# Task places shifted engine by engine, and the value products of two quads issued back to back

## The chip, the cores and the metric

The kernel runs on one core of one Trainium2 chip. The metric is the device time of one execution in microseconds (us). A core has TensorE (PE, matrix products into PSUM banks), VectorE (DVE), ScalarE (ACT), GpSimd (POOL) and SyncE (SP, which here only issues DMAs). The engines run side by side and meet through semaphores.

## The reference, cut to what matters

Two transformer layers over 8 sequences of 512 tokens, width 256, 16 heads of 16.

```python
# layer 1
q, k, v = split(x @ Wqkv);  q, k = rope(q), rope(k);  q, k = q / norm(q), k / norm(k)
x = layernorm(x + softmax(q @ k.T / 4) @ v @ Wo + bo)
# layer 2
h = layernorm(x) * ln1_w + ln1_b
x2 = x + softmax(q2 @ k2.T / 4) @ v2 @ w_proj        # q2, k2, v2 = split(h @ w_qkv)
e = argmax((layernorm(x2) * ln2_w + ln2_b) @ gate_w + gate_b)
x2 = x2 + gelu(h2 @ w1[e]) @ w2[e]                   # one expert of 8 for each token
out = layernorm(x + x2)
```

In layer 1 q and k have norm 1, so the exponentials need no maximum taken off. In layer 2 each row's largest score is found first and taken off inside the score product.

## The kernel before, in words

A sequence and a layer make a batch: batches 0 to 7 are layer 1, 8 to 15 layer 2. The program runs in 18 stages. In stage n, batch n is projected, batch n-1 attended, batch n-2 finished (output projection, norms, gate). After that a tail of 39 tiles runs the experts.

A stage has 16 quads of 4 steps; a step is written quad.step, as 5.3. In each step PE issues one score product of 128 keys by 512 queries (`score`, L417) into one of four PSUM banks (three in layer 2), and ACT takes its exponential (`exp`, L632) into `probs`. PE may issue score c only when the exponential four (in layer 2, three) steps back is done. In step 1 of every quad PE issues the value product of the quad two places earlier (`pv`, L434): four products that each use 32 columns of the array, fp32, so that the trace shows eight records for a set. All sixteen quads of a batch go to one bank, which ACT empties once in four quads (L641).

For layer 2 a maximum tile stands behind each score from quad 10 of the batch's own stage on, six quads ahead of its use: PE issues `max_score` (L449) into one of two banks and DVE reduces it (`max_tile`, L835). Every 16 tiles DVE splits the maxima into three bf16 parts (`neg_split`, L850 to L857), PE transposes them (task `NG`, L507), ACT copies them (L694), and SP sends them by DMA into the score operand (L1297). The scores of the next four quads wait for that DMA.

All else is tasks, placed by hand. The tables `PROJECTED`, `ATTENDED` and `FINISHED` give each task's (quad, step), apart for layer 1 and layer 2. At each step every engine runs its part of the tasks that stand there, behind its score, exponential or maximum; ACT runs its part one step later. The tasks that matter here:

- `T0`, `T1`: x is transposed for the projections. `qA`, `qB`, `kA`, `kB`: halves of q and k (PE L478, one PSUM bank for all projection tasks, so each waits until the one before is read out). In layer 2 ACT copies the bank to bf16 (L655) and DVE subtracts that copy from the bank (L967), which frees it.
- `sq`, `nq`, `sk`, `nk`: layer 1 only. ACT squares q or k (L664), PE sums over each head (L485), ACT takes the logarithm and the exponential of it (L671, L674).
- `mq`, `mk` (layer 2): the middle bf16 part on ACT (L680), the low part on POOL (L1182), and then 12 DMAs each on SP (L1283) that lay q and k out for the scores.
- `V0`, `V1` the values, `TO`, `TP`, `WO` the attention output, `R` the reciprocal deviations on ACT, `N1`, `N2` the norms, `HT`, `GT`, `RT` gate and routing.

Of the kernel before, what the change touches and what calls it, by code (L numbers as in the profile page):

```python
# [15 lines left out]
BATCH, T, D, H = 8, 512, 256, 16  # L16
# [38 lines left out]

PROJECTED = (
    dict(T0=(0, 0), T1=(0, 2), qA=(1, 3), qB=(2, 2), kA=(3, 3), kB=(4, 2), sq=(4, 3), nq=(5, 3),
         sk=(6, 1), uq=(6, 2), hq=(6, 3), nk=(7, 0), lq=(7, 1), uk=(8, 1), hk=(8, 2), lk=(9, 0),
         V0=(12, 0), V1=(14, 0)),
    dict(T0=(0, 0), T1=(0, 2), qA=(1, 2), qB=(2, 1), kA=(3, 0), mq=(3, 0), kB=(3, 3), mk=(4, 2),  # L60
# [5 lines left out]
    dict(TO3=(2, 3), TP0=(4, 0), TP1=(6, 3), WO0=(9, 3), WO1=(10, 2), R1=(11, 2), N10=(12, 0),  # L66
         N11=(12, 2), R2=(13, 2), N20=(14, 0), N21=(14, 2)),
    dict(TO3=(2, 3), TP0=(4, 0), TP1=(4, 3), WO0=(5, 3), WO1=(7, 0), R2=(8, 0), N20=(8, 2),
         N21=(9, 0), HT0=(10, 3), GT0=(11, 1), HT1=(12, 1), GT1=(12, 3), RT=(14, 0)))
PROJ_BANK = ("T0", "T1", "qA", "qB", "kA", "kB", "nq", "nk", "V0", "V1")  # L70
# [4 lines left out]
def second(b):  # L75
    return b >= BATCH
# [8 lines left out]
def tasks(n, q, j):  # L85

    projected, attended, finished = batches(n)
    found = []
    for b, places in ((finished, FINISHED), (attended, ATTENDED), (projected, PROJECTED)):
        if b is not None:  # L90
            found += [(name, b) for name, at in places[second(b)].items() if at == (q, j)]
    return found
# [41 lines left out]
def program(nc, x, w_qkv1, w_o1, b_o, ln1_w, ln1_b, w_qkv2, w_o2, ln2_w, ln2_b, gate_w, gate_b,  # L134
# [5 lines left out]
    with ctx:  # L140
# [193 lines left out]
        for n in range(STAGES):  # L334
            for q in range(QUADS):
                for j in range(HEADS_AT_ONCE):
                    for name, b in tasks(n, q, j):
# [48 lines left out]
        def pv_quad(n, q):  # L386

            projected, attended, finished = batches(n)
            if q < 2:
                return [] if finished is None else [(finished, QUADS - 2 + q)]  # L390
            return [] if attended is None else [(attended, q - 2)]
# [9 lines left out]
        def _(pe):  # L401
# [21 lines left out]
            def pv(b, q):  # L423

                if q == 0:
                    pe.wait_ge(*p_ring.empty(b, "V0"))
                    pe.wait_ge(*p_ring.empty(b, "V1"))
                g, kt = q // TT, q % TT
                pe.wait_ge(exps, CHUNKS * b + HEADS_AT_ONCE * (q + 1))
                if kt == 0:  # L430
                    wait(pe, oT_ready, GROUPS * b + g)
                for j in range(HEADS_AT_ONCE):
                    at = (kt * H + HEADS_AT_ONCE * g + j) * VS
# [934 lines left out]
```

## Time and profile before

| | us |
|---|---|
| median of 3 runs | 1537.66 (1533.43 to 1538.38) |
| the profiled execution, its own time | 1548.81 |
| its span, first to last instruction | 1546.8 |
| stages 2 to 7 (six, layer 1 only), each | 54.5 to 56.5 |
| stages 9 to 15 (seven, maxima in every quad), each | 78.3 to 93.1 |
| stage 16 | 67.7 |
| from the last score to the end (experts) | 371.7 |

How to read it: the stages are cut at the first score of each. A busy PE in a row counts a product from its issue to its modelled end, so the starts of two rows tell more than their lengths. "[2.12 <-DVE negm L835]" behind a row is the engine's idle time just before it and what ended it.

### The profile page before, as it was taken

What the parts mean: (1) busy time and instruction counts of PE and PEld (TensorE: products, weight loads), DVE (VectorE), ACT (ScalarE), POOL (GpSimd) and SP (SyncE); (2) the same over time, 40 slices, a digit from 0 to 9 for tenths busy, and PEclk for the clock granted to TensorE, in tenths of its full rate; (3) what the DMA queues carried; (4) which work ended last, traced back from release to release, by engine and by line L of the source; (5) the groups of instructions that cost most, each with busy time, mean ns of one, the idle gap of its engine ahead of it and who ended that gap; (6) DMA issues with size and microseconds to landing.
All of it is one profiled execution on the core that took longest, in us unless ns stands there. A gap on an engine that the chain in (4) does not pass through costs nothing. (4 is left out here: it accounts for less than half of the span.)

```text
span 1546.8 us, 20966 instructions
## 1 busy us (share of the span) xinstructions
PE 1330.6 (86%) x7238; PEld 694.1 (45%) x7238; DVE 794.6 (51%) x1815; ACT 921.1 (60%) x1617; POOL 311.7 (20%) x247
## 2 busy tenths in 40 slices
PE   3499999999998887888989899898985399999994
PEld 1223433443343323333434333333332399999993
DVE  3333553554452656566767575767761333433431
ACT  0277777787776554546556565556653167777773
POOL 4122222323321111111212121212111211111110
PEclk9699999999999998899999999999998599999997
DMA  6221431331332121112222121212236511111113
GB/s 179 81 77 47 137 94 54 127 118 59 97 123 96 42 96 42 53 45 69 69 56 83 56 83 42 96 43 83 69 111 224 170 42 53 52 52 56 52 52 129
DMA packets 103495, 127.87 MB, mean 83 GB/s; under 512 B 7168, under 2 KB 91008, under 8 KB 103264
## 3 DMA queue, kind: packets, MB, share of 16 engines
q1 hardware_dynamic: 71568, 79.45, 16.3%
q10 hardware_dynamic: 27392, 33.56, 7.3%
q0 software_dynamic: 4432, 13.52, 2.5%
q8 instruction: 60, 0.98, 0.3%
q14 instruction: 43, 0.35, 0.1%
HBM read 51.51 MB, written 28.46 MB: 52 GB/s over the span
## 5 line engine op out<-in xcount | busy, mean ns | idle before, releaser
L632 ACT ACTIVATE w_space<-bank 128x512 f32<-128x512 f32 x1024 | 565.3, 598 | 423.1 <-PE bank L417 420.1
L417 PE MATMUL bank<-w_space 96*128 96x512 bf16 (+1 forms) x1024 | 358.3, 388 | 36.3 <-DMA w_space<-neg_T 18.7
L835 DVE TENSOR_REDUCE negm<-bank 128x1 f32<-128x512 f32 x512 | 326.9, 682 | 95.6 <-PE bank L449 93.8
L434 PE MATMUL bank<-w_space 128*32 128x512 f32 x2048 | 281.4, 623 | 3.3 <-ACT w_space L641 3.3
L449 PE MATMUL bank<-w_space 96*128 96x512 bf16 x512 | 200.9, 392 | 47.0 <-DVE negm L835 40.2
L417 PEld LDWEIGHTS bank<-w_space 96*128 96x128 bf16 (+1 forms) x1024 | 94.4, 100 | 295.1 <-ACT w_space L632 176.9
L605 PE MATMUL bank<-w_space,work_space 128*128 x624 | 141.7, 380 | 0.0
L478 PE MATMUL bank<-work_space,wqkv_sb 128*128 128x512 f32 x256 | 134.7, 652 | 7.2 <-DVE w_space L962 4.8
L1182 POOL TENSOR_TENSOR work_space<-w_space,work_space 128x1024 bf16<-128x1024 f32 x32 | 68.3, 2133 | 282.0 <-ACT work_space L680 191.5
L605 PEld LDWEIGHTS bank<-w_space,work_space 128*128 128x128 f32 x624 | 115.5, 190 | 14.4
L449 PEld LDWEIGHTS bank<-w_space 96*128 96x128 bf16 x512 | 50.4, 98 | 152.5 <-DVE negm L835 115.8
L1238 POOL DMA_INDIRECT out_rows<-rows_sb,work_space x39 | 37.5, 963 | 266.8 <-DVE rows_sb L1132 266.8
L434 PEld LDWEIGHTS bank<-w_space 128*32 128x32 f32 x2048 | 40.9, 109 | 101.4 <-issue 80.3
L1216 POOL TENSOR_TENSOR row_sb<-row_sb,rows_sb 128x512 f32<-128x512 f32 x32 | 37.9, 1184 | 228.7 <-DVE row_sb L943 228.7
L592 PEld LDWEIGHTS bank<-work_space 128*128 128x128 f32 x640 | 76.7, 197 | 1.9 <-DVE work_space L1105 0.9
L592 PE MATMUL bank<-work_space 128*128 128x128 f32 x640 | 77.0, 280 | 0.5 <-DVE work_space L1105 0.5
L478 PEld LDWEIGHTS bank<-work_space,wqkv_sb 128*128 128x128 f32 x256 | 50.7, 204 | 52.5 <-issue 35.1
L967 DVE TENSOR_TENSOR w_space<-bank,work_space 128x512 f32<-128x512 f32 x32 | 22.1, 691 | 99.7 <-ACT work_space L655 99.7
L592 PEld LDWEIGHTS bank<-work_space,wqkv_sb 128*128 128x128 f32 x608 | 70.8, 192 | 1.7 <-DVE work_space L1105 0.8
L592 PE MATMUL bank<-work_space,wqkv_sb 128*128 128x128 f32 x608 | 71.1, 275 | 0.5 <-DVE work_space L1105 0.5
L1118 DVE TENSOR_TENSOR wqkv_sb<-bank,work_space 128x256 f32<-128x256 f32 x39 | 16.6, 424 | 105.0 <-PE bank L605 104.9
L492 PE MATMUL bank<-wqkv_sb,work_space 128*128 128x256 f32 x256 | 63.3, 391 | 2.7 <-DVE w_space L975 1.9
(131 smaller groups left out, 1506.9 us busy)
## 6 DMA issues: line engine op xcount, KB each, us to landing
w_space<-work_space SPq DMA_DIRECT2D x384, 128.0 KB
w_space<-in_w_dram ACTq DMA_DIRECT2D x16, 1024.0 KB, 8.4
work_space<-rows_dram SPq DMA_DIRECT2D x39, 256.5 KB, 2.6
work_space<-in_x_dram ACTq DMA_DIRECT2D x16, 512.0 KB, 3.9
x_dram<-xo SPq DMA_DIRECT2D x16, 256.0 KB, 4.7
h_dram<-row_sb SPq DMA_DIRECT2D x16, 256.0 KB, 2.3
work_space<-h_dram ACTq DMA_DIRECT2D x8, 512.0 KB, 4.1
work_space<-x_dram ACTq DMA_DIRECT2D x8, 512.0 KB, 5.5
```

The source lines that it names most:

```text
L417: nc.tensor.matmul(bank[:, :], k_stack[0:rows, b % 2, HEADS_AT_ONCE * g + j, kt * P:(kt + 1) * P], q_stack[0:rows, b % 2, HEADS_AT_ONCE * ...
L434: last = nc.tensor.matmul(pv_bank[VW * j:VW * (j + 1), :], v_aug[:, b % 2, at:at + VW], probs[:, q % PROBS, j, :], start=(kt == 0), stop=( ...
L449: nc.tensor.matmul(mx_ring.bank(b, (g, c))[:, :], q_stack[0:STACK, b % 2, h, qt * P:(qt + 1) * P], k_stack[0:STACK, b % 2, h, :], start=Tr ...
L478: last = nc.tensor.matmul(bank[:, :], wqkv_sb[:, second(b), k, c * P:(c + 1) * P], xT[:, k, :], start=(k == 0), stop=(k == KD - 1))
L492: last = nc.tensor.matmul(bank[:, j * D:(j + 1) * D], xT[:, k, tt * P:(tt + 1) * P], wqkv_sb[:, second(b), k, 2 * D:3 * D], start=(k == 0) ...
L592: last = nc.tensor.matmul(psum[2 * (j % 2) + n][:, f * P:(f + 1) * P], w1_tile[j % 2][:, k, at:at + P], xsT[:, j % 2, k, :], start=(k == 0 ...
L605: last = nc.tensor.matmul(psum[5 + j % 2][:, 0:D], hidT[:, j % 2, k, :], w2_sb[:, bass.ds(e, 1), k, :].rearrange("p a d -> p (a d)"), star ...
L632: nc.scalar.activation(probs[:, q % PROBS, j, :], st_bank(b, c)[0][:, :], ACT.Exp, scale=SCALE).then_inc(exps, 1)
L835: ve.tensor_reduce(negm[:, c % TT, c // TT:c // TT + 1], mx_ring.bank(b, (g, c))[:, :], axis=AX.X, op=ALU.max, negate=True).then_inc(mx_ri ...
L1182: pool.tensor_tensor(parts[:, qk, 2, :, :], rest[:, qk, :, :], parts[:, qk, 1, :, :], ALU.subtract).then_inc(parts_ready, 1)
L1216: pool.tensor_tensor(both, both, rows_sb[:, r:r + 1, :].to_broadcast([P, 2, D]), ALU.mult).then_inc(hw_step, 1)
L1238: pool.indirect_dma_start(out_rows, bass.IndirectOffsetOnAxis(rows_in[:, j % ROWS_AHEAD, 2 * D:ROW].bitcast(U32), 0), o_sb[:, s, :], None) ...
```

## The change

Three things change.

First, `tasks` takes a table of lags for the engine that asks, and a task may be placed in the stage before or behind its own (the loops run from -1 to 18). ACT's lag of one step is now written as a table. In layer 2 DVE runs its part of `qA`, `qB`, `kA`, `kB` three steps behind the table's place, and SP its part of `mk` three steps behind.

Second, places move. Layer 1: `sq`, `sk`, `R1`, `R2` one step earlier. Layer 2: `T0`, `T1` into quads 14 and 15 of the stage before; `qA` 1.2 to 0.2, `qB` 2.1 to 1.3, `kA` 3.0 to 3.1, `kB` 3.3 to 4.3, `mk` 4.2 to 6.0.

Third, `pv` takes a pair of quads. It stands in quads 1, 3, 5, ... 15 and issues both sets without anything between them.

```diff
-    dict(T0=(0, 0), T1=(0, 2), qA=(1, 2), qB=(2, 1), kA=(3, 0), mq=(3, 0), kB=(3, 3), mk=(4, 2),
+    dict(T0=(-2, 2), T1=(-1, 2), qA=(0, 2), qB=(1, 3), kA=(3, 1), mq=(3, 0), kB=(4, 3), mk=(6, 0),
...
+ACT_LAG = (dict(other=1), dict(other=1))
+DVE_LAG = (dict(other=0), dict(qA=3, qB=3, kA=3, kB=3, other=0))
+SP_LAG = (dict(other=0), dict(mk=3, other=0))
...
-            if q < 2:
-                return [] if finished is None else [(finished, QUADS - 2 + q)]
-            return [] if attended is None else [(attended, q - 2)]
+            if q == 1:
+                return [] if finished is None else [(finished, QUADS // 2 - 1)]
+            return [] if attended is None or q % 2 == 0 else [(attended, (q - 3) // 2)]
...
-                g, kt = q // TT, q % TT
-                pe.wait_ge(exps, CHUNKS * b + HEADS_AT_ONCE * (q + 1))
+                for q in (2 * pair, 2 * pair + 1):
+                    g, kt = q // TT, q % TT
+                    pe.wait_ge(exps, CHUNKS * b + HEADS_AT_ONCE * (q + 1))
```

The line numbers of the changed kernel are higher by 8 to 12: scores are L427, value products L445, maxima L461 (PE) and L843 (DVE), the subtraction L975, the layout DMAs L1291, the DMAs of the maxima L1305.

PE, layer 1, quads 5 to 7, from one value product over `nq` (head_sum_sb), `TP1` (on) and `nk` to the next ones. Before:

```order
L434 MATMUL bank<-w_space 32x512 x4
L417 MATMUL bank<-w_space 128x512 x2
L485 MATMUL bank<-work_space,head_sum_sb 128x512 x2
L417 MATMUL bank<-w_space 128x512 x2
L434 MATMUL bank<-w_space 32x512 x4
L417 MATMUL bank<-w_space 128x512 x2
L515 MATMUL bank<-ident_sb,on 128x128 x4
L417 MATMUL bank<-w_space 128x512
L485 MATMUL bank<-work_space,head_sum_sb 128x512 x2
L417 MATMUL bank<-w_space 128x512
L434 MATMUL bank<-w_space 32x512 x4
```

Now:

```order
L445 MATMUL bank<-w_space 32x512 x8
L427 MATMUL bank<-w_space 128x512 x2
L497 MATMUL bank<-work_space,head_sum_sb 128x512 x2
L427 MATMUL bank<-w_space 128x512 x4
L527 MATMUL bank<-ident_sb,on 128x128 x4
L427 MATMUL bank<-w_space 128x512
L497 MATMUL bank<-work_space,head_sum_sb 128x512 x2
L427 MATMUL bank<-w_space 128x512
L445 MATMUL bank<-w_space 32x512 x8
```

The set of four value products that stood between `nq` and `nk` has gone behind `nk`.

DVE, layer 2, quads 0 to 3 of a stage, from the task of the attention output (recip, on) over the first two subtractions (w_space<-bank,work_space) and the split of the maxima. Before:

```order
L990 TENSOR_TENSOR on<-bank,recip 128x4x64
L835 TENSOR_REDUCE negm<-bank 128x1 x7
L967 TENSOR_TENSOR w_space<-bank,work_space 128x512
L835 TENSOR_REDUCE negm<-bank 128x1
L850 CAST neg_parts<-negm 128x4x4
L852 TENSOR_TENSOR neg_rest<-negm,neg_parts 128x16
L855 CAST neg_parts<-neg_rest 128x4x4
L857 TENSOR_TENSOR neg_parts<-neg_rest,neg_parts 128x4x4
L835 TENSOR_REDUCE negm<-bank 128x1 x2
L967 TENSOR_TENSOR w_space<-bank,work_space 128x512
```

Now:

```order
L998 TENSOR_TENSOR on<-bank,recip 128x4x64
L843 TENSOR_REDUCE negm<-bank 128x1 x6
L975 TENSOR_TENSOR w_space<-bank,work_space 128x512
L843 TENSOR_REDUCE negm<-bank 128x1 x2
L858 CAST neg_parts<-negm 128x4x4
L860 TENSOR_TENSOR neg_rest<-negm,neg_parts 128x16
L863 CAST neg_parts<-neg_rest 128x4x4
L865 TENSOR_TENSOR neg_parts<-neg_rest,neg_parts 128x4x4
L843 TENSOR_REDUCE negm<-bank 128x1 x3
L975 TENSOR_TENSOR w_space<-bank,work_space 128x512
```

On DVE the subtractions hardly move (1.2 to 1.1, 2.1 to 2.2). What has moved is the product that they read, three steps ahead of them on PE.

SP in a layer 2 stage, the layout DMAs (w_space<-work_space) and those of the maxima (w_space<-neg_T), over two stages. Before:

```order
L1297 DMA w_space<-neg_T 3x4x512 x2
L1283 DMA w_space<-work_space 8x16x512 x24
L1297 DMA w_space<-neg_T 3x4x512 x4
L1283 DMA w_space<-work_space 8x16x512 x24
L1297 DMA w_space<-neg_T 3x4x512 x4
```

Now:

```order
L1305 DMA w_space<-neg_T 3x4x512 x2
L1291 DMA w_space<-work_space 8x16x512 x12
L1305 DMA w_space<-neg_T 3x4x512
L1291 DMA w_space<-work_space 8x16x512 x12
L1305 DMA w_space<-neg_T 3x4x512 x3
L1291 DMA w_space<-work_space 8x16x512 x12
L1305 DMA w_space<-neg_T 3x4x512
```

The third DMA of the maxima (`NG2`) now stands between the 12 of `mq` and the 12 of `mk`.

## Rows read from the trace of the kernel before

**Rows 1.** Page, part 1: busy time, share of the span, instructions.
```profile
PE 1330.6 (86%) x7238; PEld 694.1 (45%) x7238; DVE 794.6 (51%) x1815; ACT 921.1 (60%) x1617; POOL 311.7 (20%) x247
```

**Rows 2.** Windows: stretch, length, busy time by engine, clock; stages 2-7, 13, 15, tail.
```profile
123.22:454.05 330.83, 318.14 (x1683) 130.65 (x1682) 165.77 (x396) 250.54 (x481) 96.31 (x65) 0.99 0.29 94
...
864.33:946.40 82.07, 74.20 (x383) 30.34 (x382) 55.42 (x125) 46.97 (x89) 15.84 (x14) 0.96 0.21 65
...
1029.11:1107.45 78.34, 70.77 (x381) 29.49 (x382) 54.75 (x124) 46.69 (x88) 15.58 (x14) 1.00 0.20 62
...
1175.15:1546.80 371.65, 305.36 (x2023) 280.63 (x2015) 132.80 (x327) 214.27 (x279) 50.35 (x53) 0.91 0.28 87
```

**Rows 3.** Timeline, stage 5: start, length, instruction, count, idle time before it.
```profile
309.30 1.07 PE L434 MATMUL bank<-w_space 128*32 128x512 f32 x8
...
310.30 0.60 PE L417 MATMUL bank<-w_space 96*128 96x512 bf16 x2
...
311.15 1.96 PE L485 MATMUL bank<-work_space,head_sum_sb 128*128 128x512 f32 x4 [0.24 <-ACT work_space L664]
...
316.06 1.06 ACT L664 ACTIVATE work_space<-w_space 128x1024 f32<-128x1024 f32 x1
...
317.26 1.10 PE L485 MATMUL bank<-work_space,head_sum_sb 128*128 128x512 f32 x2 [1.53 <-ACT work_space L664]
```

**Rows 4.** Timeline of PE, end of stage 16: one set of value products, then two sets.
```profile
1172.64 1.07 PE L434 MATMUL bank<-w_space 128*32 128x512 f32 x8
...
1174.61 1.92 PE L434 MATMUL bank<-w_space 128*32 128x512 f32 x16
```

**Rows 5.** Waits over the whole span: total, times, longest.
```profile
DVE w_space L967 <- ACT work_space L655: 99.7, 32, 7.5
...
PE bank L449 <- DVE negm L835: 40.2, 44, 2.1
...
PE bank L417 <- DMA w_space<-neg_T: 18.7, 11, 4.7
```

**Rows 6.** Timeline, stage 13, quads 1 and 2.
```profile
873.88 0.38 PE L417 MATMUL bank<-w_space 99*128 99x512 bf16 x1
...
874.39 0.60 ACT L655 ACTIVATE work_space<-bank 128x512 bf16<-128x512 f32 x1
...
875.03 0.69 DVE L967 TENSOR_TENSOR w_space<-bank,work_space 128x512 f32<-128x512 f32 x1 [2.85 <-ACT work_space L655]
...
876.37 0.61 PE L449 MATMUL bank<-w_space 96*128 96x512 bf16 x1 [2.12 <-DVE negm L835]
```

**Rows 7.** Timeline of PE, first score of stage 4.
```profile
234.21 0.52 PE L417 MATMUL bank<-w_space 96*128 96x512 bf16 x1 [1.87 <-issue]
```

**Rows 8.** Windows behind four waits of PE: length, busy times, clock third from the end.
```profile
234.30:237.70 3.40, 3.40 (x14) 1.17 (x13) 0.69 (x1) 1.19 (x2) 0.00 (x0) 0.50 0.50 175
317.20:320.60 3.40, 3.34 (x15) 1.05 (x16) 1.87 (x4) 2.51 (x5) 1.45 (x1) 1.00 0.00 0
568.80:575.60 6.80, 4.37 (x14) 1.05 (x15) 1.38 (x2) 1.24 (x3) 0.00 (x0) 0.50 0.13 47
...
876.10:882.80 6.70, 6.43 (x18) 2.16 (x19) 2.12 (x7) 0.00 (x0) 0.00 (x0) 0.50 0.01 2
```

**Rows 9.** Timeline, stage 13, quad 6.
```profile
902.60 1.06 PE L434 MATMUL bank<-w_space 128*32 128x512 f32 x8
...
903.51 0.40 DVE L850 CAST neg_parts<-negm 128x16 bf16<-128x16 f32 x1
...
904.68 0.38 PE L507 MATMUL bank<-ident_bf,neg_parts 128*12 128x128 bf16 x4 [1.02 <-DVE neg_parts L857]
```

**Rows 10.** Timeline, stage 13, SP's DMA issues (SPq) and the score of step 8.0.
```profile
892.76 16.39 SPq L1283 DMA_DIRECT2D w_space<-work_space  x24
909.20 0.76 SPq L1297 DMA_DIRECT2D w_space<-neg_T  x1
...
912.49 0.39 PE L417 MATMUL bank<-w_space 99*128 99x512 bf16 x1 [0.69 <-DMA w_space<-neg_T]
```

## What I predict, and why

> **What bounds the kernel now.** I read the totals first, then the windows by stage, then the timelines around PE's longest waits. PE is busy for 86% of the span [rows 1]. In the six stages 2 to 7 it is busy for 318.1 of 330.8 us, at clock 0.99 [rows 2], and ACT for 250.5: layer 1 is bound by PE, and what counts there is how long each set on PE takes. A stage of layer 2 takes 78.3 us (stage 15) to 82.1 (stage 13), with DVE at 55 us [rows 2]. It is bound by no one engine: PE stops for DVE and for a DMA. The waits name them, 40.2 us for a maximum tile and 18.7 us for the DMA of the maxima [rows 5]. The tail of 371.7 us [rows 2] is the experts. Nothing of it changes, and I leave it out.
>
> **Part 1, the subtraction behind its product (gain).** In stage 13 ACT copies `qA` at 874.39, and DVE, which stands at its subtraction, does it at 875.03 after 2.85 us idle, and only then the maximum behind it. PE sits from its score at 873.88 until 876.37, 2.12 us idle, since both banks of the maxima are full [rows 6]. Over the run DVE stands so for 99.7 us before its 32 subtractions [rows 5]. All seven stages 9 to 15 show this wait, with 2.11 or 2.12 us: 14.8 us. The three other subtractions have smaller ones; of the 40.2 us [rows 5] I give them 10. The product is now three or more steps ahead of its subtraction, with a pair of value products between, so the copy is ready. What is late next is DVE itself, at some 0.61 us a tile (2.47 us for four of them would be its pace), and I keep 3 us for it. Gain 22 us.
>
> **The clock behind that wait (gain).** Behind the wait of stage 13 the granted clock is 0.50 for 6.7 us [rows 8], so products run at 1.2 GHz and not at 2.4. Stage 15 has the same wait without the fall and is 82.1 - 78.3 = 3.7 us shorter [rows 2]. Stage 14 is as stage 13; stages 9, 10 and 12 have one fall of 3.4 us each, at half pace 1.7 us. Sum 3.4 + 3.4 + 5.1 = 12 us.
>
> **Part 2, the DMA of the maxima ahead of mk (gain).** SP issues the 24 layout DMAs in one run from 892.76 to 909.15, and only then the DMA of the third group (`NG2`); the score of step 8.0 waits for it until 912.49 [rows 10]. The waits at step 8.0 are 4.7, 2.5, 1.3, 0.6, 0.7, 1.2 and 0.7 us in stages 9 to 15, 11.8 us of the 18.7 [rows 5]. With `NG2` before the twelve of `mk` it is issued some 8 us earlier, so all of it goes: 11.5 us. Behind the two longest the clock is 0.50 for 6.8 us each [rows 8]; PE is partly idle there, so I take 5 us for both.
>
> What that costs: the twelve DMAs of `mk` leave later. They take half of 16.4 us, 8.2, and the last of them lands about 3.3 us after its issue if it does as that of the maxima (909.20 to 912.49) [rows 10]. Quad 10 needs them. Counted from `WO0` at 5.3, I put SP's start at 7.5 us (DVE's sum, POOL's sum and low part, then `NG2`), so 7.5 + 8.2 + 3.3 = 19.0, and PE's arrival at 10.0 at 21. It fits with 2 us to spare, at nothing. If PE came as early as its bare sets allow, at about 18.4, it would wait 0.6 us a stage.
>
> `T0` and `T1` go to quads 14 and 15. In quad 14 PE already waits for DVE, so `T0` (0.44 us) is free there; 3 us in all.
>
> **Part 3, the pairs.** A single set starts at 309.30 and the next score at 310.30 [rows 3]; the step into it costs another 0.09 over the normal 0.22. So it takes 1.09 us of PE. In stage 16 two sets happen to stand together: 1.92 us against 1.07, the second one costs 0.85 [rows 4]. A pair saves 0.24 us where PE is what bounds. The Trainium skill, "TensorEngine Tiling (Array Packing)", Key Properties, says that a change of tiling mode drains the array. The trace agrees with 1.00 against 0.85; taken alone, the rule would promise 128 x 0.24 = 31 us, and I take less, because of the following.
>
> The pair leaves every even quad without a value product, and in some of them the single one lay in a wait. Layer 1: between `nq` at 311.15 and `nk` at 317.26 PE waits 1.53 us for ACT's square [rows 3]. `nk` can't start before that square, which now comes one exponential (about 0.5 us) earlier: 5.6 us behind `nq` and not 6.1. The value set has left that stretch, so PE waits about 1.53 + 1.09 - 0.5 = 2.1 to 2.2 us, and pays 0.85 for it later. Net cost 0.4. In quads 7 to 9 there is too little else and ACT (0.49 us for one exponential of a run) binds: cost 0.5. The six other pairs gain 6 x 0.24 = 1.4, and the 0.24 us wait of `nq` goes [rows 3]. Net gain 0.9 us a stage, 7 us for eight.
>
> Layer 2: in quad 6 the split on DVE is started at 903.51 and `NG2` waits for it until 904.68, 1.02 us behind the value set [rows 9]. Without the set it still starts then, after 2.0 us of idle PE, and the set is paid again in quad 7: 0.85. Quads 10 and 14 have a split as well: 0.8 each. Five pairs gain 5 x 0.24 = 1.2. Net cost 1.3 us a stage, 11 us for eight and a half.
>
> **Part 4, the clock behind the new waits (cost).** No row shows the new waits; these are the nearest. The wait of 1.53 us in layer 1 keeps its clock at 1.00 [rows 8] in all of stages 2 to 7. The one of 1.87 us at the start of stage 4 [rows 7] is followed by 0.50 for 3.4 us [rows 8], and of 14 waits of 1.87 us or more before 1130 us, 11 are, for 3.4 or 6.8 us. The new waits of 2.1 and 2.0 us lie with these. Fifteen of them (seven in layer 1, eight in layer 2) at 11 in 14 are 12 falls of about 2.5 us; from that 29 us I take 20, since in quad 6 and 7 of layer 2 DVE holds PE back anyway. Bounds: 0 (no fall) and 15 x 3.4 = 51 us (each one long and PE bound throughout). The Trainium skill, "TensorE: Matmul & The Clock Gate", in the section on oscillation, tells of kernels in which short bursts between waits make the array start slow each time. The falls in these rows agree with it, and the sum does not need it.
>
> **Sum.** -22 - 12 - 11.5 - 5 - 3 + 11 - 7 = -49.5 without new falls, +20 with them: -29.5. From the profiled execution, 1548.8 - 29.5 = 1519.3. The median of the runs is 11.1 us lower than that execution: 1508 us.
>
> **Rivals.** (A) The new waits leave the clock alone, as the 2.12 us of stage 15 did, or turn out shorter: -49.5, so 1488 us. For it: three of 14 waits. Against: eleven. (B) Slower: the clock. Not one but several even quads of each stage (6, 10 and 14 in layer 2, 6 and 7 in layer 1) now hold a wait near 2 us, and a fall of 6.8 us costs 3.4. It decides from 49.5 / 3.4 = 15 long falls on; at 23 it stands at -49.5 + 78, so 1566 us. For it: 6.7 us at 0.50 in stages 13 and 14. Against: DVE's pace, which hides a slow product in layer 2, and the waits that go. (C) `mk` is late at 10.0 by 2 us in eight stages: 1508 + 16 = 1524 us. For it: the margin of 2 us; against: PE slows in the same quads. (D) DVE binds layer 2: with maxima, splits and sums DVE is at 55 of 78 us [rows 2], and in quads without value products PE can be no more than two tiles ahead of it. Then the waits only change places, and the time is that of before, 1538 us. (E) The pair doesn't save what the two sets of rows 4 show, because another quad's weights have to come: 100 pairs at 0.2 less: 1528 us.
>
> **How the numbers follow.** Forecast, with some falls (1495 to 1520): 0.38. A: 0.30. C: 0.07. E: 0.05. D: 0.06. B: 0.14. I predict 1508 us. The range goes from 10 us under A, 1478, to just over D, 1540; what it leaves out is most of B and a little below A. A measurement of this kernel can tell about 0.3% from no change. Faster by more than that: forecast, A, C and E, 0.80; within it: D, 0.06; slower: B, 0.14.
>
> **What would show it.** In the profile of the changed kernel: no wait for a maximum near 2 us in quad 2 and none for the DMA of the maxima at step 8.0; DVE's idle time before the subtraction down from 99.7 us to under 20; two sets of value products in 1.92 us; `nk` about 5.6 us behind `nq` with 2.1 us idle before it; `NG2` behind 2 us of idle; the clock at 0.50 for 3.4 us or more behind about twelve of these. Stages of layer 1 should take 53 to 55 us and stages 11 to 15 76 to 79. It is wrong if the clock falls in every stage (B), if quad 10 waits for `mk` (C), or if layer 2 stages stay at 80 with DVE waiting for nothing (D).

## The result, and the profile after

| | before | after |
|---|---|---|
| median of 5 runs each | 1535.2 (1528.19 to 1538.38) | 1545.88 (1544.61 to 1547.21) |
| ratio, 95% interval | 1 | 1.0075 [1.0047, 1.0104] |
| span of the profiled execution | 1546.8 | 1544.0 |
| stage 5 (layer 1) | 54.5 | 57.4 |
| stages 11 to 15 (layer 2), each | 78.3 to 82.7 | 78.9 to 80.6 |

The kernel became 0.75% slower, some 11 us, where I had predicted 1508 us and a range from 1478 to 1540. The profiled execution of before was 14 us above this median, so the two spans hide the loss; I go by stages and by medians. Page of after, part 1, then its windows (stages 2 to 7, 13, 15 and the tail; columns as in [rows 2]):

```profile
PE 1314.5 (85%) x7238; PEld 716.5 (46%) x7238; DVE 802.6 (52%) x1815; ACT 913.6 (59%) x1617; POOL 311.4 (20%) x247
```

```profile
125.28:467.87 342.59, 319.45 (x1690) 139.91 (x1688) 162.98 (x396) 250.15 (x483) 97.90 (x66) 0.98 0.28 92
866.23:945.45 79.22, 70.23 (x384) 31.29 (x382) 56.92 (x124) 46.05 (x89) 15.81 (x14) 0.98 0.23 68
1026.00:1104.87 78.87, 69.40 (x376) 30.63 (x373) 56.69 (x124) 45.66 (x88) 15.52 (x14) 0.98 0.21 60
1173.27:1544.00 370.73, 304.78 (x2029) 280.27 (x2027) 133.29 (x328) 215.36 (x281) 51.16 (x54) 0.91 0.28 88
```

The six stages of layer 1 grew from 330.8 to 342.6 us [rows 2]. Stage 1, also of layer 1, grew by 4.2. Stages 9 to 15, in which the sum had its gains, went from 582.6 to 564.0, 18.6 less, and stages 8 and 16 grew by 2 us each. The tail is as before. What was to leave did leave. Waits of after over the whole span (total, times, longest):

```profile
PE bank L519 <- DVE neg_parts L865: 33.0, 17, 3.8
PE bank L461 <- DVE negm L843: 31.4, 46, 1.7
...
PE bank L497 <- ACT work_space L676: 17.7, 8, 2.5
...
DVE w_space L975 <- ACT work_space L667: 16.5, 4, 5.2
...
PE bank L427 <- DMA w_space<-neg_T: 2.5, 3, 1.4
```

DVE's idle time before the subtractions is 16.5 us and not 99.7, the scores' wait for the DMA of the maxima 2.5 and not 18.7 [rows 5]. SP's issues in stage 13 show why: the DMA of the third group now goes out ahead of the twelve of `mk`.

```profile
884.20 7.99 SPq L1291 DMA_DIRECT2D w_space<-work_space  x12
902.85 0.76 SPq L1305 DMA_DIRECT2D w_space<-neg_T  x1
903.71 8.50 SPq L1291 DMA_DIRECT2D w_space<-work_space  x12
```

In their place stands 33.0 us for the split (L519 is the transpose of `NG`). Of it 22.8 are one wait of 3.8 us in each of stages 10 to 15, at step 6.1; the others are shorter, as 0.59 us at 10.1. Timeline of after, stage 13, quad 6 (start, length, instruction, idle time before it):

```profile
896.73 1.26 POOL L1201 TENSOR_TENSOR row_sb<-work_space,xo 128x512 f32<-128x512 f32 x1 [12.55 <-DVE xo L1012]
...
897.64 0.38 DVE L858 CAST neg_parts<-negm 128x16 bf16<-128x16 f32 x1
...
898.28 2.14 POOL L1190 TENSOR_TENSOR work_space<-w_space,work_space 128x1024 bf16<-128x1024 f32 x1 [0.29 <-ACT work_space L692]
898.48 1.98 DVE L865 TENSOR_TENSOR neg_parts<-neg_rest,neg_parts 128x16 bf16<-128x16 f32 x1
...
900.60 0.58 PE L519 MATMUL bank<-ident_bf,neg_parts 128*12 128x128 bf16 x4 [3.80 <-DVE neg_parts L865]
```

The last instruction of the split, 16 elements a partition, takes 1.98 us. In quad 2 of the same stage it takes 0.17. It ends at 900.46, 0.04 us behind POOL's low part of `mk` (898.28 + 2.14 = 900.42), beside which the change has put it. PE waits 3.80 us, where I had expected 2.0.

Layer 1, stage 5: the read-out of `qA` by DVE and the next product, then quads 5 to 7.

```profile
303.63 0.68 DVE L970 TENSOR_TENSOR w_space<-bank,sin_sb 128x512 f32<-128x512 f32 x1
304.36 0.30 PEld L490 LDWEIGHTS bank<-work_space,wqkv_sb 128*128 128x128 f32 x2 [1.23 <-DVE w_space L970]
304.36 1.98 PE L490 MATMUL bank<-work_space,wqkv_sb 128*128 128x512 f32 x4 [0.73 <-DVE w_space L970]
```

```profile
315.50 1.92 PE L445 MATMUL bank<-w_space 128*32 128x512 f32 x16
317.36 0.61 PE L427 MATMUL bank<-w_space 96*128 96x512 bf16 x2
317.80 1.88 PE L497 MATMUL bank<-work_space,head_sum_sb 128*128 128x512 f32 x4
...
323.34 3.35 PE L497 MATMUL bank<-work_space,head_sum_sb 128*128 128x512 f32 x4 [2.14 <-ACT work_space L676]
...
329.82 2.06 PE L427 MATMUL bank<-w_space 96*128 96x512 bf16 x6
```

A pair takes the 1.92 us of [rows 4]. `nk` stands 5.54 us behind `nq` after 2.14 us of idle PE, as predicted; new is the 0.73 us at `qB`, in a quad that has lost its value set, and that the six scores at 329.82 come at 0.34 us each and not at 0.22. Quad 10 does not wait for `mk` in any stage, so the margin of 2 us held and case C did not come. Windows of 3.4 us behind the new waits (the clock is third from the end; I call a stretch at 0.50 a fall): behind `nk` in stage 5, behind the wait of 3.80 us in stage 13, and behind `nk` in stage 4.

```profile
323.30:326.70 3.40, 3.36 (x5) 1.12 (x5) 2.34 (x6) 1.84 (x4) 0.98 (x1) 0.57 0.00 0
900.60:904.00 3.40, 3.40 (x11) 1.66 (x12) 2.54 (x5) 2.08 (x4) 0.00 (x0) 0.50 0.00 0
267.80:271.20 3.40, 3.40 (x21) 0.90 (x20) 2.04 (x5) 2.96 (x7) 1.28 (x1) 1.00 0.02 5
```

### The profile page after: what moved, and what is told of

Same layout as the page of the kernel before. It is cut to its first block and busy times, and to the rows that moved or that the text cites. A ratio compares the mean times of both kernels' runs of the same rounds, so it can differ in the third digit from the quotient of the medians.

```text
span 1544.0 us, 20966 instructions
## 1 busy us (share of the span) xinstructions
PE 1314.5 (85%) x7238; PEld 716.5 (46%) x7238; DVE 802.6 (52%) x1815; ACT 913.6 (59%) x1617; POOL 311.4 (20%) x247
## 5 line engine op out<-in xcount | busy, mean ns | idle before, releaser
L843 DVE TENSOR_REDUCE negm<-bank 128x1 f32<-128x512 f32 x512 | 329.7, 684 | 143.1 <-PE bank L461 142.5
L427 PE MATMUL bank<-w_space 96*128 96x512 bf16 (+1 forms) x1024 | 357.9, 392 | 23.1 <-DMA w_space<-work_space 13.6
L445 PE MATMUL bank<-w_space 128*32 128x512 f32 x2048 | 254.2, 615 | 0.0
L461 PE MATMUL bank<-w_space 96*128 96x512 bf16 x512 | 202.6, 396 | 40.2 <-DVE negm L843 31.4
L427 PEld LDWEIGHTS bank<-w_space 96*128 96x128 bf16 (+1 forms) x1024 | 97.6, 100 | 216.4 <-ACT w_space L644 90.0
L490 PE MATMUL bank<-work_space,wqkv_sb 128*128 128x512 f32 x256 | 127.2, 620 | 13.5 <-DVE w_space L970 12.4
L461 PEld LDWEIGHTS bank<-w_space 96*128 96x128 bf16 x512 | 50.4, 98 | 149.8 <-DVE negm L843 110.2
L445 PEld LDWEIGHTS bank<-w_space 128*32 128x32 f32 x2048 | 54.7, 112 | 131.4 <-issue 104.9
L1190 POOL TENSOR_TENSOR work_space<-w_space,work_space 128x1024 bf16<-128x1024 f32 x32 | 68.2, 2131 | 212.5 <-ACT work_space L692 110.7
L490 PEld LDWEIGHTS bank<-work_space,wqkv_sb 128*128 128x128 f32 x256 | 47.0, 195 | 67.3 <-issue 39.1
L534 PE MATMUL bank<-wo_sb,w_space 128*128 128x256 f32 x256 | 70.8, 426 | 2.4 <-ACT neg_T L706 0.9
L604 PEld LDWEIGHTS bank<-work_space,wqkv_sb 128*128 128x128 f32 x608 | 70.8, 192 | 1.7 <-DVE work_space L1113 0.8
```

Of the source, the lines that this page charges most:

```text
L427: nc.tensor.matmul(bank[:, :], k_stack[0:rows, b % 2, HEADS_AT_ONCE * g + j, kt * P:(kt + 1) * P], q_stack[0:rows, b % 2, HEADS_AT_ONCE * ...
L445: last = nc.tensor.matmul(pv_bank[VW * j:VW * (j + 1), :], v_aug[:, b % 2, at:at + VW], probs[:, q % PROBS, j, :], start=(kt == 0), stop=( ...
L461: nc.tensor.matmul(mx_ring.bank(b, (g, c))[:, :], q_stack[0:STACK, b % 2, h, qt * P:(qt + 1) * P], k_stack[0:STACK, b % 2, h, :], start=Tr ...
L490: last = nc.tensor.matmul(bank[:, :], wqkv_sb[:, second(b), k, c * P:(c + 1) * P], xT[:, k, :], start=(k == 0), stop=(k == KD - 1))
L534: last = nc.tensor.matmul(bank[:, t * D:(t + 1) * D], onT[:, u, t, k, :], wo_sb[:, second(b), k, :], start=(k == 0), stop=(k == KD - 1))
L604: last = nc.tensor.matmul(psum[2 * (j % 2) + n][:, f * P:(f + 1) * P], w1_tile[j % 2][:, k, at:at + P], xsT[:, j % 2, k, :], start=(k == 0 ...
```

## The experiments

The two things that the change does, the new places with their lags and the pairs, were run apart first. Then each suspected wait was taken away. Each ratio is to the kernel before on the same chip, in four groups of runs on four chips. The medians of the kernel before were 1540.4 to 1542.2 us there, with single runs from 1526 to 1556, and 1535.2 in the test above. So a difference between two medians of different groups, or one with the changed kernel, can be some us off, and a ratio is known to 0.3 to 0.8%. Where the two disagree I give both.

### New places and lags, single value sets

```diff
 (the changed kernel, but with)
-                            for b, pair in pv_pair(n, q):
-                                pv(b, pair)
+                            for b, quad in pv_sets(n, q):
+                                pv(b, quad)
```

`pv_sets` has a flag for each layer: single sets, one in every quad as before, or pairs. Here both layers have single sets.

> The change without its third part: places and lags as in the changed kernel, but one set of value products in every quad, as before. Theory (the single set in the even quads covered waits: of the projection bank in quads 2 and 4, of ACT's square in quad 7, of the split of the maxima in quad 6): a stage of layer 1 goes from 57.4 us in the changed kernel to 54 (before: 54.5), the wait before nk from 2.14 to about 1.05, with no fall of the clock behind it; in layer 2 the wait before the third transposition goes from 3.8 to 2.7 and stages 11 to 15 from 79.7 to about 77. Total about 1545.9 - 24 - 16 = 1506 us. Rival (pairing is free, the new places themselves are what costs): the time stays at 1540 to 1550 us.

Measured 1502.91 us (1493.43 to 1507.58), ratio 0.9714 [0.965, 0.9778]. By the ratio the places and lags alone are worth 44 us (37.5 by the medians of this group). A stage of layer 1 takes 53.5 us, 1.0 less than before. Timeline of PE in its stage 5, a value set between `nq` and `nk`:

```profile
307.16 1.07 PE L453 MATMUL bank<-w_space 128*32 128x512 f32 x8
...
310.35 1.96 PE L504 MATMUL bank<-work_space,head_sum_sb 128*128 128x512 f32 x4 [0.93 <-ACT work_space L683]
```

The wait for ACT's square is 0.93 us, and no clock falls behind it in any stage. The wait at step 6.1 of layer 2 is there as well, 2.83 us (3.00 in stage 11): 3.80 less most of a value set. So it comes from the places, and the pairs only lengthen it.

### The kernel before, with pairs

```diff
 (the kernel before, but with)
+            if attended is not None:
+                sets += [(attended, q - 3), (attended, q - 2)] if q > 1 and q % 2 else []
```

> The kernel before with the third part alone: two sets of value products in every second quad, all tasks at their old places. Theory: layer 1 stages near 57.5 us (waits of 0.7 us in quad 2, over 2 us before nk, half clock behind it), layer 2 stages some 1.5 us longer than before with the waits of 2.1 us in quad 2 still there: 1535 + 24 + 10 = about 1570 us. Rival (the pair saves 0.24 us each and only the new places cost): 1535 - 15 = 1520 us.

Measured 1599.55 us (1598.31 to 1603.7), ratio 1.0358 [1.0299, 1.0417]: 55 us by the ratio, 59 by the medians, where I expected 35. `nk` waits 2.63 us here, since `sk` stands one step later, and in all six stages 2 to 7 the clock is at 0.50 for 3.4 us behind it. In layer 2 the waits of 2.12 us at step 2.1 and 2.00 us at 6.1 come together in each stage; the clock stands at half for 106 us of stages 2 to 15, and for 58 us in the kernel before.

### Pairs in layer 2 alone

```diff
 (places and lags as changed; the first of each two flags is layer 1)
-                if (False, False)[second(attended)]:
+                if (False, True)[second(attended)]:
```

> The changed kernel with pairs in layer 2 only; layer 1 has one set in every quad. Theory (the cost of the pairs adds up by stage: 57.4 against 53.5 us in layer 1, seven stages; 79.7 against 77.1 in stages 11 to 15): layer 1 stages 53.5 us, layer 2 as in the changed kernel; 1503 + 13 to 18 = 1516 to 1521 us, of the 43 us some 27 lie in layer 1. Rival (the cost lies in the waits of layer 2, 3.8 us and the clock behind it, and layer 1's part is small): 1535 us or more.

Measured 1520.32 us (1512.62 to 1522.56), ratio 0.9845 [0.9781, 0.991]. With the run of single sets and the changed kernel it divides the price of the pairs: 1520.3 - 1502.9 = 17 us for layer 2 and 1545.9 - 1520.3 = 26 us for layer 1. The ratios give 20 and 35 us.

### The wait at nk, filled

```diff
+                    for k in range(2 if name == "nk" else 0):
+                        nc.tensor.matmul(bank[:, :], head_sum_sb[:, :], cos_sb[:, :],
+                                         start=True, stop=True)
```

The two products more go to the bank that `nk` then overwrites.

> The changed kernel, with two products more before nk waits for ACT's square (0.86 us each, written to nk's own bank and overwritten by it; nothing of the result depends on them). Theory (the fall of the clock behind the wait of 2.14 us costs 1.65 us a stage, as quad 7 takes 9.0 us with it and 7.4 without): no fall in layer 1, all of stages 1 to 7 at 55.8 us, about -8 us: 1538 us. Rival (the clock falls there for another reason, or the fall costs nothing): quad 7 stays at 9.0 us, 1546 us.

Measured 1544.29 us (1539.49 to 1551.08), ratio 1.0011 [0.9982, 1.0041], 0.6% under the changed kernel by the ratios. Timeline of PE, stage 5, the two products and `nk`:

```profile
318.11 1.98 PE L496 MATMUL bank<-cos_sb,head_sum_sb 128*128 128x512 f32 x4
320.20 1.98 PE L500 MATMUL bank<-work_space,head_sum_sb 128*128 128x512 f32 x4
```

No clock falls, quad 7 takes 7.30 us in every stage where it took 9.00 with a fall and 7.37 without, and a stage takes 55.74. So the fall costs 1.65 us a stage. The rest, 55.74 against 53.5, is the pairs without any fall. The time as a whole does not settle what four such falls cost (6.6 us by the stages): it is 1.6 us less by the medians and 10 by the ratios. In the profiled execution PE also stood 2.6 and 1.7 us at the end of stages 3 and 6, for nothing that the profile shows.

### The tasks of layer 1 moved into the quads without value sets

```diff
-    dict(T0=(0, 0), T1=(0, 2), qA=(1, 3), qB=(2, 2), kA=(3, 3), kB=(4, 2), sq=(4, 2), nq=(5, 3),
-         sk=(6, 0), uq=(6, 2), hq=(6, 3), nk=(7, 0), lq=(7, 1), uk=(8, 1), hk=(8, 2), lk=(9, 0),
+    dict(T0=(0, 0), T1=(0, 3), qA=(1, 1), qB=(3, 0), kA=(3, 3), kB=(5, 1), sq=(4, 2), nq=(6, 1),
+         sk=(6, 2), uq=(7, 0), hq=(7, 1), nk=(7, 1), lq=(7, 2), uk=(8, 2), hk=(8, 3), lk=(9, 1),
```

Pairs in layer 1, single sets in layer 2, the middle part of `mk` one step later on ACT (below).

> As single_mk_later, but with pairs in layer 1, and layer 1's tasks moved so that a pair stands between a product and the next one that needs its bank, and between ACT's square and nk (T1 0.3, qA 1.1, qB 3.0, kA 3.3, kB 5.1, nq 6.1, nk 7.1 and what follows them). Theory (pairs cost in layer 1 only because the waits lost their cover): stages 2 to 7 at 52 to 53.5 us, so 0 to 10 us faster than single_mk_later. Rival (pairs starve ACT, whose exponentials bind in quads without much else, wherever the tasks stand): stages 2 to 7 at 55 us or more, 10 us or more slower than single_mk_later.

Measured 1503.83 us (1502.15 to 1511.96), ratio 0.9763 [0.9701, 0.9825], and 1485.17 with single sets. A stage of layer 1 takes 55.55 us, still 2 more than with single sets, and 57.21 in the two in which the clock falls. The waits for read-outs are gone or short, but there are others. Timeline of PE in one stage:

```profile
319.45 1.96 PE L504 MATMUL bank<-work_space,head_sum_sb 128*128 128x512 f32 x4 [0.51 <-ACT work_space L683]
...
324.04 1.36 PE L436 MATMUL bank<-w_space 96*128 96x512 bf16 x3 [1.11 <-ACT w_space L651]
```

The second is a score that waits for ACT's exponential. A quad without a value set and without a task takes PE 4 x 0.22 = 0.9 us and ACT 2.0, four exponentials at 0.49: PE runs four scores ahead and stands. The theory that better places would let the pair pay fell for these places, the only ones tried; the rival held.

### ACT's middle part of mk one step later

```diff
-ACT_LAG = (dict(other=1), dict(other=1))
+ACT_LAG = (dict(other=1), dict(mk=2, other=1))
```

POOL's low part waits for that middle part (898.28, `[0.29 <-ACT work_space L692]`), so this starts it behind the split. First in the changed kernel, with its pairs:

> The changed kernel, with ACT's part of mk one step later (6.2 in place of 6.1), so that POOL's low part of k starts after DVE's split of the maxima is done. Theory (DVE's fourth instruction of the split takes 1.98 us in place of 0.17 because POOL's instruction runs at the time): that instruction goes back to 0.17 us in stages 10 to 15, PE's wait before the third transposition from 3.8 to about 2.0 us, 1.8 x 6 = 11 us and up to 6 us from shorter falls of the clock: 1530 to 1535 us. Rival (DVE is late there for its own work, or the DMAs of mk come too late for quad 10): the wait before the third transposition stays at 3.8 us, or a new wait stands at quad 10, and the time stays at 1546 us.

Measured 1538.11 us (1530.24 to 1541.99), ratio 0.9962 [0.9927, 0.9998]. That is 8 us under the changed kernel by the medians and 17 by the ratios; I had expected 11 to 16. Then with single sets:

> The respaced kernel with one set in every quad, with ACT's part of mk one step later. Theory (POOL's instruction holds DVE's fourth instruction of the split for 1.8 us, here as in the changed kernel): the wait before the third transposition goes from 2.83 to 1.0 us, no fall of the clock behind it, stages 11 to 15 from 77.1 to 74 us: 1503 - 12 to 18 = 1485 to 1491 us. Rival (with the set still in quad 6 the wait is hidden or comes back at quad 10, where the DMAs of mk land): 1503 us.

Measured 1485.17 us (1480.63 to 1487.78), ratio 0.9618 [0.956, 0.9676], 17.7 us less (15 by the ratios). The split's last instruction and PE behind it, stage 13 with single sets:

```profile
846.39 0.17 DVE L872 TENSOR_TENSOR neg_parts<-neg_rest,neg_parts 128x16 bf16<-128x16 f32 x1
...
846.71 0.38 PE L526 MATMUL bank<-ident_bf,neg_parts 128*12 128x128 bf16 x4 [1.02 <-DVE neg_parts L872]
```

The wait at 6.1 is 2.00 us with pairs (3.80) and 1.02 with single sets (2.83), and only `mk` was moved: POOL's 2.14 us held the split. The other side of it stands in quad 10, stage 13:

```profile
863.62 0.59 PE L468 MATMUL bank<-w_space 96*128 96x512 bf16 x1 [1.58 <-DMA w_space<-work_space]
```

With single sets the layout of k now comes 0.8 to 2.0 us late in stages 10 to 15, the prediction's case C; with pairs it does not.

### SP's lag for mk taken back

```diff
-SP_LAG = (dict(other=0), dict(mk=3, other=0))
+SP_LAG = (dict(other=0), dict(other=0))
```

> The respaced kernel with one set in every quad, but SP's part of mk not three steps later, so its twelve DMAs stand ahead of the DMA of the third group of the maxima. Theory (that order is what made PE wait at step 8.0): a wait at 8.0 for the DMA of the maxima of 3 us or more comes back in stages 9 to 15, since mk now leaves later than in the kernel before; 1503 + 20 to 40 us. Rival (the wait at 8.0 went because PE comes later): no wait there, 1503 us.

Measured 1532.35 us (1525.99 to 1543.8), ratio 0.9936 [0.9902, 0.997]; 29 us are lost against single sets with the lag (34 by the ratios). Waits of PE's scores for the DMA of the maxima, of this kernel and of the one with the lag:

```profile
PE bank L436 <- DMA w_space<-neg_T: 28.5, 13, 8.0
```

```profile
PE bank L436 <- DMA w_space<-neg_T: 8.3, 5, 2.4
```

This is more than the 18.7 us of [rows 5]: `mk` itself stands later than in the kernel before, so its DMAs hold that of the maxima longer.

### DVE's lag of three steps taken back

```diff
-DVE_LAG = (dict(other=0), dict(qA=3, qB=3, kA=3, kB=3, other=0))
+DVE_LAG = (dict(other=0), dict(other=0))
```

> The kernel with the new places and lags and one set of value products in every quad (1502.91 us in its runs), with DVE's lag of three steps for the four subtractions behind the projections set to 0. That undoes Part 1 of the prediction alone. Theory (the lag is what took PE's wait for a maximum tile in quads 0 to 4 away): a PE wait of about 2 us for a maximum tile stands again in quads 1 to 3 of each stage of layer 2, DVE is idle 2 to 3 us ahead of its subtractions, and the time is 15 to 30 us more, 1518 to 1533. Rival (the products' own earlier places are enough, since ACT's copy comes one step behind them in any case): no new wait of PE over 0.6 us, within 5 us of 1503.

Measured 1538.68 us (1532.08 to 1551.74), ratio 0.9981 [0.9942, 1.0021]: 36 us are lost against single sets (41 by the ratios), over the 15 to 30 that the theory gave. Its waits, and the first of three in stage 13:

```profile
DVE w_space L982 <- ACT work_space L674: 92.7, 32, 4.3
...
PE bank L468 <- DVE negm L850: 42.7, 38, 1.7
```

```profile
854.51 0.39 PE L468 MATMUL bank<-w_space 96*128 96x512 bf16 x1 [1.63 <-DVE negm L850]
```

These are nearly the 99.7 and 40.2 of [rows 5] again. That PE gives the product earlier is not enough; DVE has to come to its subtraction later than ACT's copy.

### kB and mk earlier, so that POOL is done before the split

```diff
-    ... kA=(3, 1), mq=(3, 0), kB=(4, 3), mk=(6, 0),
+    ... kA=(3, 1), mq=(3, 0), kB=(4, 1), mk=(5, 0),
...
-SP_LAG = (dict(other=0), dict(mk=3, other=0))
+SP_LAG = (dict(other=0), dict(mk=6, other=0))
```

Single value sets.

> The same single-set kernel, with the second keys' product and the layout task mk moved up in layer 2 (kB two steps, mk from 6.0 to 5.0), so that GpSimd's low part of mk ends before DVE's split begins, and with SyncE's lag of mk at six steps, so that its twelve DMAs still stand behind that of the third group of maxima. Theory (DVE's fourth instruction of the split is held until GpSimd's low part ends, and the mk DMAs come late only because that low part was moved back): the instruction takes about 0.17 us instead of 1.98, the wait of PE at step 6.1 is 1.0 us and not 2.8, no half clock behind it, and no wait at 10.0 over 0.3 us; 1472 to 1480 us. Rival 1 (the hold goes with the split itself, whatever GpSimd does): the wait at 6.1 stays 2.8 us, 1500 us. Rival 2 (SyncE's 24 issues in a row, and not GpSimd, set when mk lands): the wait at 10.0 stays 1.2 to 1.6 us, 1485 us.

Measured 1473.74 us (1468.2 to 1477.07), ratio 0.9554 [0.9475, 0.9633]. Timeline of stage 13, quads 5 and 6:

```profile
833.91 2.13 POOL L1197 TENSOR_TENSOR work_space<-w_space,work_space 128x1024 bf16<-128x1024 f32 x1 [9.01 <-ACT work_space L699]
...
837.23 0.40 DVE L865 CAST neg_parts<-negm 128x16 bf16<-128x16 f32 x1
...
838.08 0.17 DVE L872 TENSOR_TENSOR neg_parts<-neg_rest,neg_parts 128x16 bf16<-128x16 f32 x1
...
838.40 0.38 PE L526 MATMUL bank<-ident_bf,neg_parts 128*12 128x128 bf16 x4 [1.02 <-DVE neg_parts L872]
```

POOL's part ends at 836.04, ahead of the split, whose last instruction takes 0.17 us. The wait is 1.02 us, nothing waits at 10.0, stages 12 to 14 take 72.9 us each and no clock falls in stages 10 to 15. With neither the hold nor the late layout the time is 29 us under single sets at the places of the change (25 by the ratios).

### The same, and nk behind a value set

```diff
-         sk=(6, 0), uq=(6, 2), hq=(6, 3), nk=(7, 0), lq=(7, 1), ...
+         sk=(6, 0), uq=(6, 2), hq=(6, 3), nk=(7, 1), lq=(7, 2), ...
```

> The run before with one more step: in layer 1 the task nk one step later (7.1 for 7.0), and lq behind it, so that the single set of value products of quad 7 stands between nq and nk. Theory (a value set in a wait costs nothing, and one outside it costs its 1.09 us): the wait of 0.93 us ahead of nk goes, each stage 2 to 7 is 0.7 to 0.9 us shorter, together 5 to 7 us under the run before. Rival (ACT's exponentials bind in quads 7 to 9 of layer 1 and the time only changes place): within 1.5 us of the run before.

Measured 1469.26 us (1467.88 to 1484.71), ratio 0.9518 [0.9445, 0.9591]. The wait of 0.93 us is gone, but a stage takes 53.22 and not 53.5: quad 7 is 1.0 us shorter, quads 8 and 9 are 0.7 longer. That is 0.28 us a stage and not the 0.7 to 0.9 of the theory, so mostly the rival; the medians, 4.5 us apart, lie within each other's spread. This is the best version, some 4.8% under the kernel before.

### Pairs in layer 2, with kB and mk early

> The kernel with single sets, kB and mk moved up and SyncE's lag of six for mk (1473.74 us in its runs: its stages 12 to 14 take 72.9 us and no clock falls there), with the value products of layer 2 alone in pairs. It measures the pairs of layer 2 by themselves, with the hold by GpSimd and the falls of the clock out of the way. Prediction's Part 3: net cost 1.3 us a stage, 8.5 stages, 11 us, 1485 us. Rival (a pair saves nothing in any quad, since in the quad without a set PE runs two maximum tiles ahead of DVE and stands, 0.4 to 0.9 us in quads 0, 4, 8 and 14 by the trace of the changed kernel, and pays both sets behind it; in the kernels with single and paired sets already run, the quads other than 6 and 7 differ by 3.3 us a stage): stages 12 to 14 take 3.3 us more plus 1.0 at step 6.1, 77 us, 4.2 x 8 = 34 us, and with the value set gone from it the wait at 6.1 is 2.0 us; 1500 to 1508 us. If the clock falls behind that wait, up to 1.7 us a stage more, 1520 us at most.

Measured 1505.62 us (1493.6 to 1508.24), ratio 0.9751 [0.9705, 0.9797]: 32 us for the pairs of layer 2 alone, where Part 3 of the prediction gave 11. Windows of stage 12 of this kernel, and of stage 13 with single sets, both with the clock at 1.00:

```profile
754.88:831.18 76.30, 69.08 (x383) 30.62 (x381) 54.91 (x124) 45.92 (x89) 15.79 (x14) 1.00 0.24 70
```

```profile
806.62:879.52 72.90, 70.06 (x383) 29.65 (x381) 55.27 (x124) 46.40 (x89) 15.79 (x15) 1.00 0.24 74
```

PE is busy for 1 us less and the stage is 3.4 us longer. By pairs of quads (0 and 1, 2 and 3, and so on) the difference is +0.4, +0.1, +0.45, +0.4, +0.4, +0.7, 0.0 and +1.0 us: it is in no place less than nothing. Stage 13, quad 8 of the pairs, PE and then DVE:

```profile
874.71 0.39 PE L468 MATMUL bank<-w_space 96*128 96x512 bf16 x1 [0.68 <-DVE negm L850]
```

```profile
873.97 1.88 DVE L850 TENSOR_REDUCE negm<-bank 128x1 f32<-128x512 f32 x3
```

And with single sets, where the set stands between the same tiles:

```profile
846.32 1.07 PE L453 MATMUL bank<-w_space 128*32 128x512 f32 x8
847.32 0.39 PE L436 MATMUL bank<-w_space 99*128 99x512 bf16 x1
847.54 0.38 PE L468 MATMUL bank<-w_space 96*128 96x512 bf16 x1
```

A step with a score and a maximum tile takes PE 0.44 us and DVE 0.6. In the quad without a value set PE fills both banks of the maxima and stands for DVE; with one, that time is the value set's.

## Why the prediction was wrong

**Layer 2, Parts 1 and 2: the waits right, a side effect missed.** The waits they named left, and taking either lag back costs as much as they said or more. Part 1 with its clock term gave 22 + 12 = 34 us; taking DVE's lag back costs 36. Part 2 gave 16.5; taking SP's lag back costs 29, but from a later `mk`, with 28.5 us of waits where the kernel before has 18.7, so that is not its worth against the kernel before. Together with 3 us for `T0` and `T1` the terms are 53.5. Some 6 us of Part 3 belong here as well: `nq`'s 0.24 us and the 0.5 us by which ACT's square comes earlier, in eight stages. They came true, since a stage of layer 1 with single sets is 1.0 us shorter. So the places and lags were to give 59.5 us; the run with single sets shows 44, because of the next point.

**The first missed step: what else of mk was moved.** Part 2 counted `mk`'s DMAs and their queue, and its low part on POOL, 2.14 us, only as a delay of these. It didn't ask what that instruction does to DVE beside it, and the same move set it beside the split of the third group. In its place DVE's instruction of 0.17 us takes 1.98. Moved off again, the time falls by 17.7 us with single sets (1502.9 to 1485.2; 15 by the ratios) and by some 1.1% with pairs. The trace of before had a small sign of it in a row that I quoted: the cast of 0.40 us in [rows 9], which takes 0.17 in quad 2 of the changed kernel.

**The second, Part 3, the pairs: wrong sign in layer 1, a third of the size in layer 2.** That a pair takes 1.92 us held, so case E fell. The step that failed is "the six other pairs gain 6 x 0.24", and the same for five in layer 2. I had asked only of the longest waits whether a value set lay in them. But each quad without a set has a short wait: for a read-out (0.35, 0.73 and 0.29 us in quads 0, 2 and 4 of stage 5), for exponentials behind its `nk` (329.82), for DVE's maxima in quads 0, 4, 8 and 14 of layer 2. In stages 5 and 13 of the kernel before only the last of them shows (0.62 us in quad 14), because the set covered the others. For layer 1 I gave a gain of 0.9 us a stage (its own terms add up to 0.8). Stage 5 shows a cost of 3.0, by pairs of quads +0.3, +0.75, -0.2, +2.0, +0.4, -0.2, 0.0 and 0.0. In the +2.0 are 1.65 us of slow clock, which Part 4 counted; the rest is 1.3. The pairs by themselves, against single sets at the same places, cost 2.3 us a stage without a fall (55.8 against 53.5) and 3.9 with one. Of the seven pairs of quads other than 6 and 7 only one gained the 0.24 us: 10 and 11. For layer 2 I gave a cost of 1.3 a stage, and it is 3.4.

**The sum.** Parts 3 and 4 gave the pairs 4 + 20 = 24 us, or 30 without the 6 us of the moves. Measured are 1545.9 - 1502.9 = 43 us by the medians, and 56 by the ratios. By the ratios the forecast misses by 41 us: 26 of them are the pairs (56 against 30), 15 the places and lags (44 against 59.5), which is what POOL's hold on the split costs. By the medians it misses by 38, 13 and 25 (the hold 18). Both steps failed by either count; how the miss divides between them is not known better than this.

**Part 4, the clock: right in kind.** I had gone by 11 falls for 14 waits. Waits of PE at `nk` and at step 6.1 in stages 2 to 15, and how many had a fall that began between the wait's start and 2.5 us behind its end (each lasts 3.4 or 6.8 us), in all the traces:

| wait | falls |
|---|---|
| 0.93 at `nk`, seven kernels with single sets in layer 1 | 0 of 42 |
| 1.02 at 6.1, the kernel before and four with single sets in layer 2 | 0 of 30 |
| 1.53 at `nk`, kernel before | 0 of 6 |
| 2.00 at 6.1, pairs in layer 2, kB and mk early | 3 of 6 |
| 2.00 at 6.1, `mk` later on ACT, pairs | 5 of 6 |
| 2.00 at 6.1, kernel before with pairs | 5 of 6 |
| 2.14 at `nk`, changed kernel, and with `mk` later | 4 of 6 each |
| 2.63 at `nk`, kernel before with pairs | 6 of 6 |
| 2.82 to 3.00 at 6.1, three kernels with single sets | 17 of 18 |
| 3.80 at 6.1, changed kernel and two others | 18 of 18 |

So in the changed kernel 10 of 12 such waits have their fall, about the share forecast. The time went the way of case B, slower, but not by its mechanism: the changed kernel stands at half clock for 65 us of stages 2 to 15, the kernel before for 58, and the 7 us more cost 3.5 at most. The Trainium skill, "TensorE: Matmul & The Clock Gate", "A second HAM failure mode: psum-queue depth-cycling", tells of a kernel in which short idle times between groups of products send the clock back and forth. The table agrees with it from the waits of 2.00 us on; its waits up to 1.53 us left the clock alone.

**Case D in part.** It named what holds in the quads without value products: PE is no more than two tiles ahead of DVE. I gave it 0.06 and no price by quads. By the quads above, this is where most of the pairs' cost in layer 2 stands; no run takes that wait away by itself.

**What stays open.** Single waits of 1.6 to 6.0 us between two stages, for nothing that the profile shows, as 234.21 in [rows 7]. They stand ahead of stage 4 in four of the 14 traces and ahead of stage 7 in two, and no run here isolates them. Whether other places in layer 1, with `nk` filled, would let the pairs pay was not tried.

## What to carry to other kernels

Before work is drawn together to save a switch, look at each place that it leaves, not only at the longest wait: a short set between two dependent steps covers a wait that the trace doesn't show while it is covered. When a task is moved, follow its instruction on every engine to its new neighbours, those on GpSimd above all, since a small VectorE instruction beside it can take ten times as long (0.17 us became 1.98 here). And test the parts of a change apart: by the ratios one part was worth 44 us here and the other cost 56.

## What the hardware showed that I had not expected

DVE's small instructions from SBUF waited for POOL's large one. The `TENSOR_TENSOR` with two SBUF inputs took 1973 to 1975 ns in all six of stages 10 to 15 of the changed kernel, each ending 0.03 us behind POOL's L1190; elsewhere 0.17. The cast with one fp32 SBUF input took 0.38 to 0.39 us beside L1201 and 0.36 beside another of POOL's, again ending 0.03 us behind it, and 0.39 to 0.50 in 13 of 32 cases in the kernel before. A reduction from a PSUM bank that began while L1190 ran kept its usual 0.68 us, in eight cases.

The second cast of the split starts within 16 ns of POOL's low part in 36 cases of six traces. In 30 of them it takes 0.17 us and the instruction behind it is held, as above. In the other six the cast itself is held for all of POOL's instruction, and the one behind it takes 0.17 again. Stage 11 with single sets (the wait of 3.00 us):

```profile
708.10 2.14 DVE L870 CAST neg_parts<-neg_rest 128x16 bf16<-128x16 f32 x1
708.10 2.12 POOL L1197 TENSOR_TENSOR work_space<-w_space,work_space 128x1024 bf16<-128x1024 f32 x1 [0.27 <-ACT work_space L699]
```

The Trainium skill, "SBUF — State Buffer", "Who interferes with whom", states this: DVE and GpSimd share a pair of ports, whichever starts first holds it for its whole instruction, and DVE needs it with two SBUF inputs or in a 2-port mode. The rows on DVE agree with it; which mode the casts ran in no row shows. A prediction that had asked this of the moved `mk` would have found the hold, and with it the 15 to 18 us.
